# Output projection in front of the last softmax tail, additions of the time mix on TensorE, a receptance by chunks in the channel mix, and two of four reciprocals as a power on GpSimd

## The reference, cut to what matters

```
x = x + L1_xattn(layernorm(x), ctx_1024)      # 16 heads, 1601 keys, relative terms, softmax
        # ... (w1 + w2) @ Wo + bo
x = x + L1_attn(layernorm(x)):
    xa = ln(x, ln1_g, ln1_b);  xx = shift(xa)             # one token back
    xk, xv, xr = xa * mix + xx * (1 - mix)                # three mixes
    k, v, r = xk @ Wk.T, xv @ Wv.T, xr @ Wr.T
    # scan over the tokens, with running maxima pp:
    out = (e1 * aa + e2 * vv) / (e1 * bb + e2)            # num / den
    x = x + (sigmoid(r) * out) @ Wo.T
    xc = ln(x, ln2_g, ln2_b)                              # channel mix
    kk = square(relu(xk2 @ ffn_Wk.T))
    x = x + sigmoid(xr2 @ ffn_Wr.T) * (kk @ ffn_Wv.T)
```

## Time and profile before

| | us |
|---|---|
| median of three runs | 1625.36 (1620.1 to 1625.64) |
| the profiled execution's own time | 1619.36 |
| its span in the trace | 1617.2 |
| TensorE busy in it | 1440.0 (89 %) |
| VectorE, ScalarE, GpSimd busy | 726.2, 496.3, 517.0 |

### The profile page before, as it was taken

One profiled execution on the slowest core, in us unless ns is written; L12 is line 12 of the kernel. 1 busy time (PEld: TensorE's weight loads), 2 busy tenths in 40 slices (PEclk: granted clock), 3 DMA queues, 4 the chain that ended last, 5 costly groups with the idle time before them and its releaser, 6 DMA issues. The chain is left out here.

```text
span 1617.2 us, 26502 instructions
## 1 busy us (share of the span) xinstructions
PE 1440.0 (89%) x11120; PEld 1059.3 (66%) x11120; DVE 726.2 (45%) x1269; ACT 496.3 (31%) x824; POOL 517.0 (32%) x296
## 2 busy tenths in 40 slices
PE   7778987457997989999999999999999998866995
PEld 3556874233443768878888888888888875423873
DVE  2454269989634533232332323323233232685822
ACT  0323312131211204324343242433334352432612
POOL 6102038756314133313223132232222302235901
PEclk9778967778997999999999999999999999977997
DMA  6300030010101421111111111111111006003000
GB/s 243 139 18 1 0 143 1 0 72 0 78 0 59 132 62 55 54 40 44 54 37 53 44 40 54 40 50 43 41 54 53 27 12 277 1 0 124 0 0 26
DMA packets 49140, 88.01 MB, mean 54 GB/s; under 512 B 28536, under 2 KB 41088, under 8 KB 45952
## 3 DMA queue, kind: packets, MB, share of 16 engines
q1 hardware_dynamic: 49024, 86.32, 15.1%
HBM read 76.61 MB, written 9.70 MB: 53 GB/s over the span
## 5 line engine op out<-in xcount | busy, mean ns | idle before, releaser
L1173 POOL TENSOR_TENSOR ctx_hi<-ctx_raw,one 128x1536 fp32r<-128x1536 f32 (+1 forms) x32 | 91.5, 2858 | 567.3 <-DMA ctx_raw<-in_ctx 325.9
L1458 DVE TENSOR_SCALAR_CACHE_REDUCE E<-PS 128x384 f32<-128x384 f32 (+1 forms) x256 | 131.8, 571 | 180.6 <-PE PS L1246 180.0
L1355 ACT COPY ET<-PS 128x512 f32<-128x512 f32 (+1 forms) x224 | 129.5, 584 | 269.1 <-PE PS L1269 194.2
L1427 DVE TENSOR_TENSOR V<-PS,vbias 128x512 f32<-128x512 f32 (+1 forms) x104 | 71.7, 691 | 193.1 <-PE PS L1213 193.0
L1213 PE MATMUL PS<-ctx_raw_r,wk_hi 128*128 128x384 f32 (+1 forms) x512 | 128.2, 355 | 0.0
L1213 PE MATMUL PS<-wv_lo,ctx_hi 128*128 128x512 f32 (+1 forms) x416 | 127.6, 406 | 0.0
L1269 PE MATMUL PS<-ident,E 128*128 128x128 f32 (+1 forms) x832 | 123.1, 273 | 2.5 <-ACT E L1362 2.5
L1362 ACT ACTIVATE E<-E,peak 128x1601 f32<-128x1601 f32 x64 | 103.5, 1623 | 66.9 <-DVE peak L1463 66.9
L1213 PE MATMUL PS<-ctx_hi,wk_hi 128*128 128x384 f32 (+1 forms) x512 | 120.6, 357 | 1.5 <-POOL ctx_raw_r L1176 1.5
L1213 PE MATMUL PS<-wv_hi,ctx_hi 128*128 128x512 f32 (+1 forms) x416 | 119.6, 409 | 0.8 <-issue 0.8
L1176 POOL TENSOR_TENSOR ctx_raw_r<-ctx_raw,ctx_hi 128x1536 fp32r<-128x1536 f32 (+1 forms) x32 | 116.8, 3651 | 2.5
(11 more groups left out here) (283 smaller groups left out, 2332.1 us busy)
## 6 DMA issues: line engine op xcount, KB each, us to landing
ctx_raw<-in_ctx SPq DMA_DIRECT2D x24, 768.0 KB, 4.4
ctx_raw<-in_ctx_first SPq DMA_DIRECT2D x8, 900.0 KB, 4.5
rel_scr<-rel_out SPq DMA_DIRECT2D x8, 640.0 KB, 3.6
fwk<-in_fwk SPq DMA_DIRECT2D x1, 4096.0 KB, 15.5
fwv<-in_fwv SPq DMA_DIRECT2D x1, 4096.0 KB, 12.3
corr<-rel_scr SPq DMA_DIRECT2D x64, 48.0 KB
p_scr<-E SPq DMA_DIRECT2D x16, 192.0 KB, 2.3
near<-p_scr SPq DMA_DIRECT2D x64, 48.0 KB
```

The source lines that it names most:

```text
L1173: nc.gpsimd.tensor_tensor(ctx_hi[r][:, :, 0:n], ctx_raw[r][:, :, 0:n], one[:].unsqueeze(1).broadcast_to([P, KC, n]), ALU.mult).then_inc(S[ ...
L1355: nc.scalar.copy(ET[0:n, j % ET_RING, :], src[0:n, :]).then_inc(S["et_out"], 1)
L1427: v.tensor_tensor(V[0:rows, at % V_RING, :], bank(4 + NUMBER[unit] % 2)[0:rows, :], vbias[0:rows, :], ALU.add).then_inc(S["v_out"], 1)
L1458: v.tensor_scalar(E[:, p, k0:k0 + n], bank(r)[:, 0:n], 1.0, None, ALU.mult, ALU.max, accum_out=tops[:, p, c:c + 1]).then_inc(S["s_out"], 1)
```

## The change

Four things change.

1. Three of the four tiles of the output projection, which need only batches 0 to 5, move into period 8 of the cross attention, at slots 4, 6 and 8, which is behind the second, third and fourth of its value units and in front of all transposes of batch 7. w3o and b3o are loaded at the start of that period, after the last scores. VectorE adds the three tiles to X, and does both of their normalisations while the tail of batch 7 runs. `cross_output` keeps the last tile.
2. In the time mix, v and r are made output by output (`linear_to_features`). The two additions of each o become products with the identity on TensorE, which sum in PSUM (`add_den`, `add_num`). VectorE takes the reciprocal of den 0 and 2 from PSUM; ScalarE copies den 1 and 3 to SBUF, and GpSimd raises them to the power of minus one, against one column of -1. num times the reciprocal is now read from PSUM on VectorE, and the product with the gate, which GpSimd made, is on VectorE too. The divisions are in another order: 0 after `sums(1)`, 1 to 3 after `sums(3)`.
3. In the normalisation behind the time mix, a tile's application comes after the next tile's moments.
4. In the channel mix the receptance takes the chunks of xr in the outer loop, each as it is ready.

```diff
+EARLY_OUTPUT = (4, 6, 8)
...
         turns, weighs = (lambda j: slots + j // 2), (lambda kt: slots + kt + 2)
-        scored, spread = (), slots + 17
+        scored, spread, order = (), slots + 17, "opltrs"
+        for tile, slot in enumerate(EARLY_OUTPUT):
+            put(slot, ("o", tile))
+            put(slots + 5 + 2 * tile, ("l", tile))
...
             for p, ba, items in PERIODS:
+                if p == B:
+                    sp.wait_ge(S["s_ps"], len(S_JOBS) * B)
+                    sp.dma_start(s.w3o[:], s.dram["w3o"]).then_inc(s.loaded["w3o"], 16)
+                    sp.dma_start(s.b3o[:], s.dram["b3o"].partition_broadcast(P)).then_inc(s.loaded["b3o"], 16)
...
-            for n in ("w3o", "b3o", "vecs", "awk", "awv", "awr", "awo", "fwr"):
-                src = s.dram[n].partition_broadcast(P) if n == "b3o" else s.dram[n]
-                sp.dma_start(s.late[n][:], src).then_inc(s.loaded[n], 16)
+            for n in ("vecs", "awk", "awv", "awr", "awo", "fwr"):
+                sp.dma_start(s.late[n][:], s.dram[n]).then_inc(s.loaded[n], 16)
...
+            pool.wait_ge(s.loaded["b3o"], 16)
+            for t in range(NT):
+                nc.gpsimd.tensor_tensor(s.X[:, t, :], s.X[:, t, :], s.b3o[:], ALU.add).then_inc(S["biased"], 1)
+            for t in range(len(EARLY_OUTPUT)):
+                after.pool(pool, t)
+                after2.pool(pool, t)
...
+            def output(t):
+                pe.wait_ge(s.loaded["w3o"], 16)
+                pe.wait_ge(S["normed"], 2 * t + 2)
+                pe.wait_ge(S["s_out"], 4 * B * len(S_JOBS))
+                if t >= 2:
+                    pe.wait_ge(S["added"], t - 1)
+                linear_to_tokens(nc, bank(2 + t % 2), s.YT, t, s.w3o, 0, D).then_inc(S["y_ps"], 1)
...
+            def add_output(t):
+                dve.wait_ge(S["biased"], t + 1)
+                dve.wait_ge(S["y_ps"], t + 1)
+                v.tensor_tensor(s.X[:, t, :], s.X[:, t, :], bank(2 + t % 2), ALU.add).then_inc(S["added"], 1)
+
+            def norms(t):
+                dve.wait_ge(S["added"], t + 1)
+                after.moments(ch, t, s.X)
+                dve.wait_ge(S["v_ps"], len(V_NTH))
+                after.apply(dve, t, s.X, s.x0)
+                dve.wait_ge(after.tile_ready, t + 1)
+                after2.moments(ch, t, s.x0)
+                after2.apply(dve, t, s.x0, s.XN)
...
@@ cross_output, TensorE and VectorE @@
-            pe.wait_ge(s.loaded["w3o"], 16)
-            for t in range(NT):
-                linear_to_tokens(nc, bank(4 + t), s.YT, t, wo, 0, D).then_inc(y_ps, 1)
+            linear_to_tokens(nc, out, s.YT, last, s.w3o, 0, D).then_inc(y_ps, 1)
...
+            dve.wait_ge(y_ps, 1)
+            nc.vector.tensor_tensor(s.X[:, last, :], s.X[:, last, :], out, ALU.add).then_inc(x_done, 1)
+            dve.wait_ge(x_done, 1)
+            nm.moments(ch, last, s.X)
+            nm.apply(dve, last, s.X, s.x0)
+            dve.wait_ge(nm.tile_ready, NT)
+            nm2.moments(ch, last, s.x0)
+            nm2.apply(dve, last, s.x0, s.XN)
...
@@ time_mix, TensorE @@
-            for i, (x, wn, done) in enumerate(((xk, "awk", "k_ps"), (xv, "awv", "v_ps"), (xr, "awr", "r_ps"))):
-                pe.wait_ge(s.loaded[wn], 16)
-                pe.wait_ge(tr.ready, KC)
-                if i == 2:
-                    pe.wait_ge(S["k_in"], KC)
-                for c in range(KC):
-                    pe.wait_ge(S["mixed"], KC * i + c + 1)
-                    for o in range(KC):
-                        last = nc.tensor.matmul(bank(4 * ((i + 1) % 2) + o), w[wn][:, c, o * P:(o + 1) * P],
-                                                x[:, c].rearrange("p b q -> p (b q)"), start=(c == 0), stop=(c == KC - 1))
-                        if c == KC - 1:
...
+            pe.wait_ge(s.loaded["awv"], 16)
+            pe.wait_ge(S["mixed"], 2 * KC)
+            for o in range(KC):
+                linear_to_features(nc, bank(o), w["awv"], o, xv[:].rearrange("p c b q -> p c (b q)")).then_inc(S["v_ps"], 1)
+            pe.wait_ge(s.loaded["awr"], 16)
+            pe.wait_ge(S["mixed"], 3 * KC)
+            pe.wait_ge(S["k_in"], KC)
+
+            def receptance(o):
+                pe.wait_ge(S["v_in"], o + 1)
+                linear_to_features(nc, bank(o), w["awr"], o, xr[:].rearrange("p c b q -> p c (b q)")).then_inc(S["r_ps"], 1)
+
+            def add(out, x, y):
+                nc.tensor.matmul(out, s.ident[:], x, start=True, stop=False)
+                return nc.tensor.matmul(out, s.ident[:], y, start=False, stop=True)
+
+            def add_den(o):
+                if o >= 2:
+                    pe.wait_ge(S["den_copied" if o % 2 else "inverted"], 1)
+                pe.wait_ge(S["exps"], 4 * o + 4)
+                pe.wait_ge(S["den_part"], o + 1)
+                add(split(bank(4 + o % 2)), den[:, o % 2], p2[:, o]).then_inc(S["den_ps"], 1)
+
+            def add_num(o):
+                if o >= 2:
+                    pe.wait_ge(S["gated"], o - 1)
+                pe.wait_ge(S["num_pool"], 2 * o + 2)
+                pe.wait_ge(S["num_part"], o + 1)
+                add(split(bank(6 + o % 2)), num[:, o], out_now[:, o, :, 1:]).then_inc(S["num_ps"], 1)
+
+            receptance(0), add_den(0), add_num(0), receptance(1), add_den(1), add_num(1), receptance(2), add_den(2)
+            receptance(3), add_num(2), add_den(3), add_num(3)
...
@@ time_mix, ScalarE @@
+            def den_copy(o):
+                act.wait_ge(S["den_ps"], o + 1)
+                nc.scalar.copy(inverse[:, o], split(bank(4 + o % 2))).then_inc(S["den_copied"], 1)
+
+            den_copy(1)
...
-                nc.scalar.activation(gate[:, o], split(bank(4 + o)), ACT.Sigmoid).then_inc(S["gate_in"], 1)
+                nc.scalar.activation(gate[:, o], split(bank(o)), ACT.Sigmoid).then_inc(S["gate_in"], 1)
+            den_copy(3)
...
@@ time_mix, GpSimd @@
+            nc.gpsimd.memset(minus_one[:], -1.0).then_inc(S["minus_one"], 1)
+
+            def invert(o):
+                pool.wait_ge(S["den_copied"], o // 2 + 1)
+                nc.gpsimd.tensor_tensor(row(inverse[:, o]), row(inverse[:, o]), minus_one[:].broadcast_to([P, TOK]), ALU.pow).then_inc(S["inverted_pool"], 1)
+
             for o in range(KC):
+                if o == 3:
+                    pool.wait_ge(S["minus_one"], 1)
+                    invert(1)
                 pool.wait_ge(S["exps"], 4 * o + 4)
                 pool.wait_ge(S["v_in"], o + 1)
                 nc.gpsimd.tensor_tensor(row(top[:, o]), row(p4[:, o]), row(vp[:, o]), ALU.mult).then_inc(S["num_pool"], 1)
                 nc.gpsimd.tensor_tensor(out_now[:, o, :, 1:], p2[:, o], vp[:, o, :, 1:], ALU.mult).then_inc(S["num_pool"], 1)
-            for o in range(KC):
-                pool.wait_ge(S["gate_in"], o + 1)
-                pool.wait_ge(S["num_done"], o + 1)
-                nc.gpsimd.tensor_tensor(gate[:, o], num[:, o], gate[:, o], ALU.mult).then_inc(S["num_gated"], 1)
+            invert(3)
...
@@ time_mix, VectorE @@
-                ch.add(v.tensor_tensor(den[:, o % 2], p1[:, o], sum_1[:, o, :, 0:SQ], ALU.mult))
+                v.tensor_tensor(den[:, o % 2], p1[:, o], sum_1[:, o, :, 0:SQ], ALU.mult).then_inc(S["den_part"], 1)
                 dve.wait_ge(S["num_pool"], 2 * o + 2)
                 ch.link(v.tensor_tensor_scan(row(sum_v[:, o]), row(p3[:, o]), row(top[:, o]), 0.0, ALU.mult, ALU.add))
-                ch.add(v.tensor_tensor(num[:, o], p1[:, o], sum_v[:, o, :, 0:SQ], ALU.mult))
-                ch.link(v.tensor_tensor(den[:, o % 2], den[:, o % 2], p2[:, o], ALU.add))
-                v.tensor_tensor(num[:, o], num[:, o], out_now[:, o, :, 1:], ALU.add).then_inc(S["num_done"], 1)
-                ch.add(v.reciprocal(den[:, o % 2], den[:, o % 2]))
+                v.tensor_tensor(num[:, o], p1[:, o], sum_v[:, o, :, 0:SQ], ALU.mult).then_inc(S["num_part"], 1)
+
+            def invert(o):
+
+                dve.wait_ge(S["den_ps"], o + 1)
+                v.reciprocal(row(inverse[:, o]), bank(4 + o % 2)).then_inc(S["inverted"], 1)
             def divide(o):
-                ch.sync()
-                dve.wait_ge(S["num_gated"], o + 1)
-                v.tensor_tensor(gate[:, o], gate[:, o], den[:, o % 2], ALU.mult).then_inc(S["gated"], 1)
+                dve.wait_ge(S["inverted_pool" if o % 2 else "inverted"], o // 2 + 1)
+                dve.wait_ge(S["num_ps"], o + 1)
+                ch.link(v.tensor_tensor(row(inverse[:, o]), bank(6 + o % 2), row(inverse[:, o]), ALU.mult))
+                dve.wait_ge(S["gate_in"], o + 1)
+                v.tensor_tensor(gate[:, o], gate[:, o], inverse[:, o], ALU.mult).then_inc(S["gated"], 1)
             for o in range(KC):
                 exponents(o)
-            for o in range(KC):
-                sums(o)
-                if o >= 1:
-                    divide(o - 1)
-            divide(KC - 1)
```

(14 more changed lines are left out.)

61 lines of the change are left out of this document (29 added, 32 removed).

## The result

| | before | after |
|---|---|---|
| median of the runs | 1622.73 us (4 runs, 1618.3 to 1625.64) | 1743.84 us (4 runs, 1743.65 to 1746.32) |
| the profiled execution, own time and span | 1619.36, 1617.2 | 1743.65, 1741.5 |
| mean granted clock | 0.925 | 0.901 |

The ratio is 1.0764, with the interval from 1.0736 to 1.0792. The forecast was 1618 with a range up to 1646: the time lies 98 us outside it, and the sign is wrong.

The account below looks back on a forecast made before the run. TensorE was taken as the bound up to 1326 us and in batch 7's tail, VectorE in the time mix's reciprocals. Terms -3.8 + 0.7 - 3.9 = -7.0 from 1625.36 gave 1618 us, range 1605 to 1646 for 8 in 10.

Parts of the forecast that it names:

- the size of p: Time mix: p, the length of one 512-column power on GpSimd, taken as 6.1 us from VectorE's reciprocal-to-product ratio.
- the power is long: Rival, time mix: p from 15 us upward, standing twice on the path; 1644 at 20 us, 1664 at 30; chance 0.25.
- Until it is over VectorE gets nowhere: Time mix: the first power blocks VectorE's gate product, with two SBUF inputs, for all of p, 6.1 us.
- 81.7: Time mix: predicted us from the start of its transposes to the first addition into x0, before 78.1.
- 1.5 for the clock: Time mix: 1.5 us added because TensorE pauses during the first power and its clock falls.
- the -7.0: Whole kernel: predicted change in us, the sum of early output, time mix and receptance terms.
- one costs two: Time mix: above p of about 8 us the second power sticks out too, so each further microsecond costs two.
- The early output, -3.8: Cross attention's end: 11.2 us saved before the time mix's transposes, 7.4 paid in batch 7's tail; -3.8 us, 1.5 either way.
- The tail, -2.9: Time mix's end: additions and moments by tiles no longer wait for the power between them; 9.5 us instead of 12.4.
- The receptance by chunks, -3.9: Channel mix: receptance starts 3.7 us sooner, without waiting for all four chunks; -3.9 us, between -3 and -5.
- The additions on TensorE: Time mix: eight additions of 1.72, 13.8 us of added TensorE work, hide in 7.5 + 6.8 us of its idleness.
- the power is hidden: Rival, time mix: VectorE goes on beside the power, only TensorE's queue counts; -15.6 us in all, 1610; chance 0.22.

Follow-up runs that it names:

- pow_by_itself: A program of its own: GpSimd powers of several widths alone, then beside VectorE's products and reciprocals, then products on both engines; 512 columns took about 81.92 us.
- cols_36: The change with each of its two powers cut to 36 of 512 columns, the rest left as denominators: 1605.37 us, ratio 0.9912 to the kernel before.
- cols_124: The change with each of its two powers cut to 124 of 512 columns, the rest left as denominators: 1622.66 us, ratio 1.0025 to the kernel before.
- pow_behind: The change with the power of den 1 moved behind GpSimd's two products for o = 3: 1744.53 us, one run.
- early_only: The kernel before with the early output projection alone, time mix and channel mix as before: 1614.61 us, ratio 0.9976.
- old_sums_c: The kernel before with early output projection, receptance by chunks and reordered tail, the time mix's sums as before: 1610.76 us, ratio 0.9943.
- all_dve: The change with all four reciprocals on VectorE from PSUM, no 512-column power, divisions reordered: 1606.89 us, ratio 0.9924 to the kernel before.
- mixed: all_dve with the additions of o = 0 on VectorE and one output projection chunk before TensorE's additions of o = 3: 1599.96 us, ratio 0.9877.
- one_pow: The change with den 1 also on VectorE, leaving only den 3 as a power, behind all of GpSimd's products: 1681.17 us, one run.

## Why the prediction was wrong, step by step

**The step that failed is "the size of p".** The prediction had bounds of 1.6 and 290 us from one power of one column and chose 6.1 by VectorE's ratio of a reciprocal to a product. Measured: 81.93 for each of the two, 75.8 more, and both lengths are on the path. The choice between ends a factor of 180 apart was made by an analogy with another engine and another operation, and nothing bore it out. There was one row for this operation on this engine, the 0.567 us of the earlier trace rows, and 0.35 of it was more than a start. Read as a price for a column, that difference gives 0.35 x 512 = 179 us; measured are 0.159 us a column and a start of 0.40 instead of 0.2. The row couldn't give p, but nothing in it spoke for 6.1 either. The rival "the power is long" stood on it, but was given 0.25 and ended at 30 us.

**"Until it is over VectorE gets nowhere" was wrong too.** The pair at 1419.76 and 1420.98 consists of two products, and two products do hold each other (pow_by_itself). A power holds VectorE only at its start: a product issued 0.03 us behind it takes 1.56 us, one issued 1.9 us into it takes 0.69, in the change and in cols_36. The rule of the Trainium skill that stood beside it ("SBUF — State Buffer", "SBUF: two separate sides": the lock is held for the whole instruction) agrees with the pairs of products (1.41 to 1.56 us instead of 0.69). It doesn't agree with a power of 512 columns, which holds for about 1 of its 82 us. At p = 6.1 cols_36 prices this step. The prediction's 81.7 is 45.6 up to the power's start, 28.5 behind it (its terms as written add up to 28.2), 6.1 for p and 1.5 for the clock; measured are 47.6 and 28.2, so neither p nor the 1.5 lay on the path. That is 5.9 us net of the 7.3 by which the kernel beat the -7.0. With p right and this step as predicted, "one costs two" above 8 would have given -5.1 + 2 x (81.9 - 8) = +143 in place of the measured +124.

**That one us costs two** held for long powers: 1.94 for one from cols_124 to the change. Its start lies nearer 11 (an estimate) than 8. The reason is that GpSimd can't start the second power before the first has ended, and `divide(3)` waits for the second. The products for o = 3 between them add a wait of their own in the trace, but pow_behind, which takes them out of the way, is no faster.

**The early output, -3.8**: met, as a mark (-3.8) and alone (-3.9, interval -6.8 to -1.0). The mark isn't sharp: in the nine kernels with the early output the stretch from the last scores to the transposes is 61.6 to 64.1 us, one execution each, against 66.2. What the sum didn't have is the k projection behind it, which takes 1.7 us longer in the change: the transposes are followed by values 20.3 us later instead of 18.6. The granted clock is 0.80 in that stretch, after 12.1 us in which TensorE was busy for 5.30. Up to the values the gain is thus 2.1 us in the change and 2.6 in early_only (4.6 up to the transposes, 2.0 given back); that the forecast is met is in part luck.

**The tail, -2.9**: 3.4 by the marks. **The receptance by chunks, -3.9**: the stretch from the end of the last application to the hidden layer is 5.5 shorter (18.5 against 24.0 us); 3.5 are the earlier start, the rest its length, 13.97 instead of the 16.00 of the earlier trace rows. The same edit shows 15.85 at a granted 0.88 in old_sums_c and 13.97 at the full clock in the change and in all_dve, so these 2 us are the clock's and not the edit's. Tail and receptance together are 7.3 shorter by the marks of old_sums_c, where 6.8 were predicted.

**The additions on TensorE** hide, as predicted, but in all_dve the time to x0 stays at 78.4: the k projection takes 2.1 us longer, and TensorE's own queue holds VectorE for 6.30 us and the output projection back behind o = 3. What that queue costs only mixed brought out.

The rival "the power is long" had the sign and the two lengths on the path, and with a p of 82 its rule would have been within 19 us; it had the gate product wait for the first power, and what waited was the scan of `sums(3)`. The rival "the power is hidden" is what cols_36 comes near: 73.1 us to the first addition against 75.8 measured, and -15.6 us in all against -14.3.

What stays open: what GpSimd does for 0.159 us a column. The runs show the same length for two exponents, for mixed values and for ones, and with and without a neighbour, not why; another type or another form of the instruction wasn't tried. Why the power holds VectorE only at its start is open too. That its time is that of one product of the same width suggests a hold while the inputs are read; no run separates that.

## What to carry to other kernels

Where the cost of an added operation has bounds a hundredfold apart, the forecast is the bounds: split the chances by where the change breaks even between them, and take the row of the same operation on the same engine, however small, before a ratio from another engine. Where an operation takes longer for one column than that engine's other operations, run it by itself at two or three widths before it is moved there: that takes one small program. And before two operations are put on an idle engine, count them as one queue: once they are longer than what covers them, each costs its whole length.

## What the hardware showed that I had not expected

- A power on GpSimd takes 0.56 us for one column of 128 rows, 2.91 for 16, 10.52 for 64 and 81.92 for 512; a product of 512 takes 1.04.
- It holds a VectorE operation with two inputs in SBUF only when that one comes at the power's start: 0.03 us behind it a product takes 1.56 us, 0.8 us behind it 0.80, and from then on 0.69; reciprocals beside it take what they take elsewhere (3.35). A product of GpSimd holds one of VectorE for its whole length (1.41 to 1.56 us for each of four that met).
- With TensorE at work for 13.58 of 81.90 us the granted clock of that stretch is 0.61, a mean between the two levels; the 24 records of the output projection behind it take 11.38 us at a granted 0.92, where they take 10.46 at the full 2.4 GHz (one_pow, cols_124).
